# A graph kernel's third mask: one VectorE pass over the adjacency becomes an accumulating transfer from GpSimd's queue

## The reference

```python
# layer 0: attention, one head: leaky_relu(s_i + t_j), masked by adj, softmax, relu
# layer 1: 8 heads of 16, scores in leaky_relu, masked by adj, softmax, elu
# layer 2: mean over the neighbours (relation 1) @ W + x @ self_w.T + b, layernorm, relu
# layer 3, 4 heads of 32:
Wh = jnp.einsum('bsf,hfd->bhsd', features, W)
scores = jnp.einsum('bhsd,bhtd->bhst', Wh, Wh) / jnp.sqrt(jnp.float32(D))
scores = jnp.where(adj_matrix[:, None, :, :] > 0, scores, NEG_INF)
attn = jax.nn.softmax(scores, axis=-1)
h = jnp.einsum('bhst,bhtd->bhsd', attn, Wh)
```

## Time and profile before

| | |
|---|---|
| median of 3 runs | 2535.16 us (2532.8 to 2535.92) |
| the profiled execution: its time, its span | 2537.21 us, 2535.5 us |
| TensorE (PE) busy | 2281.9 us, 90% of the span |
| VectorE (DVE) busy | 2173.3 us, 86% |
| ScalarE (ACT) busy | 1944.8 us, 77% |
| GpSimd (POOL) busy | 167.5 us, 7% |
| granted TensorE clock, mean | 0.965 |
| chain that ended last | PE 64%, DVE 14%, issue 9%, ACT 8%, DMA 3%, POOL 2% |

### The profile page before, as it was taken

The page is one execution under the profiler, slowest core; times in us unless marked ns, Lnnn a source line. Parts: engine busy times, 40 slices in busy tenths (PEclk is TensorE's granted clock), DMA queues, the critical chain, the costliest instruction groups (busy, mean ns, idle before and its releaser), DMA issues.

```text
span 2535.5 us, 56744 instructions
## 1 busy us (share of the span) xinstructions
PE 2281.9 (90%) x23694; PEld 1528.0 (60%) x23813; DVE 2173.3 (86%) x4125; ACT 1944.8 (77%) x2161; POOL 167.5 (7%) x104
## 2 busy tenths in 40 slices
PE   3668999989999999999989899998989999998966
PEld 3557556575765658575665757656485765657341
DVE  3688799898988989898898989889898989989756
ACT  2758798787879878787987778788787878878714
POOL 0000001001000100100010010001001000100000
PEclk9788999999999999999999999999999999999978
DMA  6504133222323322232332123233222323101000
GB/s 129 134 18 118 42 85 77 62 74 43 102 68 85 83 65 64 43 101 68 85 84 66 62 43 101 68 85 76 60 77 42 102 68 85 45 33 52 9 17 9
DMA packets 192976, 172.80 MB, mean 68 GB/s; under 512 B 137168, under 2 KB 171088, under 8 KB 191696
## 3 DMA queue, kind: packets, MB, share of 16 engines
q1 hardware_dynamic: 191424, 135.61, 19.5%
q0 software_dynamic: 1296, 33.56, 6.5%
HBM read 151.78 MB, written 42.53 MB: 77 GB/s over the span
## 4 chain that ended last, share of the span: by engine, by line
PE 64%; DVE 14%; issue 9%; ACT 8%; DMA 3%; POOL 2%; SPq 1%; POOLq 0%; ACTq 0%; DVEq 0%
PE kp L821 15%; PE kp L804 10%; PE fp L707 9%; PE fp L646 9%; PE kp L797 6%; PE kp L752 3%; DVE weight L1317 3%; ACT ramp L994 3%; DMA shared<-shared 2%; DVE bstat L1127 2%; ACT weight L1037 2%; PE kp L749 2%; POOL bsmall L541 2%; PE fp L600 2%; PE fp L593 1%
## 5 line engine op out<-in xcount | busy, mean ns | idle before, releaser
L994 ACT ACTIVATE ramp<-s1row,tbig 128x1024 bf16<-128x1024 f32 x864 | 921.0, 1143 | 85.6 <-DVE weight L1317 85.5
L1037 ACT ACTIVATE weight<-kp,shift 128x1024 f32<-128x1024 f32 x512 | 543.9, 1114 | 196.2 <-PE kp L804 194.7
L1317 DVE TENSOR_TENSOR weight<-ramp,AT 128x2048 bf16<-128x2048 bf16 x512 | 609.6, 1221 | 75.9 <-ACT ramp L994 52.1
L821 PE MATMUL kp<-weight,w 128*33 128x512 f32 x2048 | 490.9, 600 | 9.5 <-ACT weight L1037 5.7
L707 PEld LDWEIGHTS fp<-vh_parts,weight 128*128 128x128 bf16 x8192 | 402.8, 100 | 130.5 <-DVE weight L1317 66.7
L707 PE MATMUL fp<-vh_parts,weight 128*128 128x102 bf16 x8192 | 431.9, 212 | 40.0 <-DVE vh L1325 24.7
L804 PE MATMUL kp<-shared 32*128 32x512 f32 x2048 | 298.0, 652 | 9.8 <-ACT weight L1037 7.5
L821 PEld LDWEIGHTS kp<-weight,w 128*33 128x33 f32 x2048 | 97.7, 110 | 321.4 <-issue 255.9
L646 PEld LDWEIGHTS fp<-features,weight 128*128 128x128 f32 x2048 | 234.9, 194 | 40.9 <-issue 40.3
L646 PE MATMUL fp<-features,weight 128*128 128x129 f32 x2048 | 240.7, 279 | 16.9 <-DVE weight L1228 16.9
L1456 DVE SCALAR_TENSOR_TENSOR weight<-AT,weight 128x1024 f32<-128x1024 bf16 x182 | 214.6, 1222 | 36.7 <-ACT weight L1037 36.7
(11 more groups left out here) (179 smaller groups left out, 2527.3 us busy)
## 6 DMA issues: line engine op xcount, KB each, us to landing
s1row<-s_rows_dram SPq DMA_DIRECT2D x128, 512.0 KB, 4.1
adj_bf_dram<-in_adj_dram POOLq DMA_DIRECT2D x15, 2048.0 KB, 13.7
x<-in_x_dram SPq DMA_DIRECT2D x16, 512.0 KB, 7.5
xfT<-s_row_dram SPq DMA_DIRECT2D x16, 512.0 KB, 3.6
shared<-shared SPq DMA_DIRECT2D x32, 256.0 KB, 3.5
out_dram<-elu SPq DMA_DIRECT2D x16, 512.0 KB, 4.5
adj_bf_dram<-in_adj_dram POOLq DMA_DIRECT2D x2, 1024.0 KB, 10.8
s_rows_dram<-weight SPq DMA_DIRECT2D x16, 32.0 KB
```

The costliest lines, as they stand in the source:

```text
L821: last = pe.matmul(kp[side(h), 0, :], w3[:, (2 * J + x) * H3 + h, :], weight3[:, w % P_RING, x * HALF:(x + 1) * HALF], start=(J == 0 and x ...
L994: act.activation(ramp[:, u % R_RING, :], s1row[:, h % S_RING, :], ACT.Relu, bias=tbig1[:, jt, h:h + 1], scale=BIG).then_inc(ramp_ready.sem, 1)
L1037: act.activation(weight3[:, w % P_RING, :], kp[:, 1 + 2 * (w % 2):3 + 2 * (w % 2), :].rearrange("p a n -> p (a n)"), ACT.Exp, bias=shift3[ ...
L1317: dve.tensor_tensor(edges[:, u % B_RING:u % B_RING + 2, :], ramp[:, u % R_RING:u % R_RING + 2, :], AT[:, third, jt:jt + 2, :], ALU.min).th ...
```

## The change

`layer3_mask` leaves VectorE. GpSimd issues a transfer that adds a tile of -1 (`minus`, 128x256 bf16, read over and over) to the third of `AT`, in pieces of 256 elements (512 bytes), 32 for each of 128 partitions: 4096 pieces, 2 MB written. `mask3_made` counts 16 a graph. TensorE waits for it ahead of couple 0 as before. VectorE now waits for it ahead of its first masked couple. The five couples of `MASKED` stay. All five tables of steps are new. On VectorE `stats2` goes from step 16 to 17, behind one more L1317, and `relu2` from 21 to 23, behind an L1325 as well; on TensorE the first `project0` goes from step 25 to 29, behind four more pieces of layer 1, and couple 0 of the scores keeps step 49 with the same pieces ahead of it.

```diff
+        minus = sb("minus", [P, 2 * P], BF16)
...
-        mask3_made = signal("mask3_made", 1)
+        mask3_made = signal("mask3_made", 16)
...
         ON_POOL = [
-            (dict(adjacency=3, rstd0=4, rstd1=5, rstd2=0, rstd3=1, rstd_tail=2),),
+            (dict(adjacency=3, mask3=1, rstd0=5, rstd1=6, rstd2=0, rstd3=2, rstd_tail=4),),
         ]
         ON_SP = [
-            (dict(adjacency=1, far=6, out=10, sources=[2, 3, 4, 5, 7], sources_ahead=[12, 13, 14], spread_row=9,
-                 store_row=8, store_sources=11, x=0),),
+            (dict(adjacency=4, far=5, out=10, sources=[0, 2, 3, 7, 9], sources_ahead=[12, 13, 14], spread_row=8,
+                 store_row=6, store_sources=11, x=1),),
         ]
...
+            pool.memset(minus[:], -1.0).then_inc(consts_made, 1)
...
+            def layer3_mask(b, third):
+                if b == 0:
+                    pool.wait_ge(consts_made, 4)
+                pool.wait_ge(sum2_made.sem, sum2_made.of(b))
+                pool.dma_start(AT[:, third].rearrange("p t (c n) -> p (t c) n", n=2 * P),
+                               minus[:].unsqueeze(1).broadcast_to([P, T * T // 2, 2 * P]), accum_op=ALU.add) \
+                    .then_inc(mask3_made.sem, 16)
...
+                if k is not None and s == at["mask3"]:
+                    layer3_mask(k, (r + 2) % 3)
...
-            def layer3_mask(b, third):
-
-                dve.wait_ge(sum2_made.sem, sum2_made.of(b))
-                dve.tensor_scalar(AT[:, third], AT[:, third], -1.0, None, ALU.add).then_inc(mask3_made.sem, 1)
-
             def layer3_masked(b, third, v):
...
+                    if w == 2 * masks(b)[0]:
+                        dve.wait_ge(mask3_made.sem, mask3_made.of(b))
```

More of the change, by code:

```diff
@@ L390, in graph_stack @@
         ON_PE = [
[L391 to L396, removed]
+            (dict(maxima1=93, maxima3=44, project0=[29, 31, 35], project1=91, project2=102, project3=42, scores3=[49,
+                 53, 56, 58, 64, 70, 74, 83, 85, 87, 90, 94, 98, 101, 104, 106], self2=5, self_weights=73, shift3=48,
+                 sources1=95, spread0=47, spread1=96, sum1=[18, 20, 23, 25, 26, 27, 37, 38], sum2=[0, 1, 3, 8, 9, 13,
+                 15, 16], top0=41, turn0=[17, 24], turn1=89, turn2=99, turn3=39, turn_back=30, unit0=[72, 75, 76, 78,
+                 79, 80, 81, 82], unit1=[2, 4, 6, 7, 10, 11, 12, 14, 19, 21, 22, 28, 32, 33, 34, 36, 40, 43, 45, 46,
+                 50, 51, 52, 55, 59, 60, 62, 63, 65, 66, 67, 69], values3=[54, 57, 61, 68, 71, 77, 84, 86, 88, 92, 97,
                  100, 103, 105, 107, 108]),),
@@ L399, in graph_stack @@
         ON_ACT = [
[L400 to L405, removed]
+            (dict(cut1=[81, 82], cut1_second=[87, 91], elu=66, exp3=[31, 32, 34, 36, 38, 39, 41, 42, 47, 48, 53, 54,
+                 57, 58, 62, 63, 64, 65, 68, 69, 71, 72, 74, 75, 78, 79, 84, 85, 88, 89, 92, 93], exps0=35, exps1=77,
+                 first2=86, out3=[49, 67, 83, 96], prepare0=46, project0=[16, 18, 20], project1=73, project3=26,
+                 ramps=[0, 1, -1, 2, 3, 4, -1, 5, 6, 8, 9, 11, 13, 14, 15, 19, 21, 22, 28, -1, 29, 30, -1, 33, 37, -1,
+                 40, 43, 44, 45], ramps_ahead=[94, 95], second2=90, self2=7, sources1=76, sum1=[17, 23, 24],
+                 turn0=[10, 12], turn1=70, turn2=80, turn3=25, unit0=[50, 51, 52, 55, 56, 59, 60, 61], wide3=27),),
@@ L406, in graph_stack @@
         ]
         ON_DVE = [
[L408 to L414 removed]
+            (dict(affine2=20, columns1=[91, 92], cut1=[94, 96], cut1_third=[99, 102], divide1=81, elu1=84, finish0=82,
+                 finish1=69, finish3=25, head1=[7, 13, 21, 29, 40, 49, 56, 62], lengths3=34, low2=101, masked3=[55,
+                 61, 65, 66, 70, 71, 72, 74, 75, 76, 85, 90, 93, 95, 98, 100], maxima1=87, maxima3=36, maximum0=39,
+                 most0=33, norm0=83, norm1=88, norm3=27, out2=15, prepare=68, ramps=[2, 9, 35, 44, 51], relu2=23,
+                 residual3=46, rest2=97, shift0=57, shift3=38, shifts1=89, stats2=17, tail3=60, top0=28, top1=86,
+                 unit0=[63, 64, 67, 73, 77, 78, 79, 80], unit1=[0, 1, 3, 4, 5, 6, 8, 10, 11, 12, 14, 16, 18, 19, 22,
+                 24, 26, 30, 31, 32, 37, 41, 42, 43, 45, 48, 50, 52, 53, 54, 58, 59], z0=47),),
@@ L1519, in step @@
                     layer3_residual(m)
-                if k is not None and s == at["mask3"]:
-                    layer3_mask(k, (r + 2) % 3)
                 for v in range(PAIR_UNITS):
```

7 lines of the change are left out of this document (removed).

## The result

| | before | after |
|---|---|---|
| median (lowest to highest, runs) | 2535.54 us (2532.8 to 2538.62, 4) | 2622.14 us (2620.03 to 2636.01, 4) |
| ratio to before, with its interval | 1 | 1.0353 [1.0315, 1.0391] |
| span of the profiled execution, mean granted clock | 2535.5 us, 0.965 | 2622.3 us, 0.948 |
| from the first power of layer 2 to the second, start to start | 12.32 us | 15.10 us |

The change costs 86.6 us; the forecast was 2616 us.

A forecast was written before the change was run, and what follows sets the result against it. TensorE was taken to set the time, with the landing of `spread_far` as hinge. 13 x 6.5 = 84.5 us of collision less 3.3 us of gain gave +81 us, 2616 us for the median; range 2518 to 2690 us.

The forecast's parts named there:

- What bounds the kernel: TensorE sets the time, busy 140.5 of 147 us; a later landing of `spread_far` lengthens the period by as much.
- The pass filled a hole, 0.1 us a period: VectorE without its 2.30 us mask pass would wait for ScalarE's copy `w3`, winning only 0.1 us a period.
- The new order gains at most 15 us: TensorE reaches layer 2's result sooner: 1.1 us usable in each of some 14 full periods.
- The issue, 8 us and free up to 12.7 us: GpSimd issues the mask's 4096 pieces in about 8 us; only time over 12.7 us holds VectorE at `layer2_norm`.
- X = 20 us: Duration of the mask's transfer on the DMA engines, landing 9.6 us ahead of couple 0, so TensorE doesn't wait.
- The cast queues behind the mask and reaches into `spread_far`: Load of the next adjacency, behind the mask on its queue, makes `spread_far` land 4.8 us late; chance 0.50.
- 6.5 us in 13 periods, 84.5 us: Cost of the late `spread_far`: 4.8 us of delay plus 1.7 us of lower clock in each period with a load.
- The row load and the store and spread of layer 0's row, nothing: These transfers, in the same stretch as `spread_far`, were costed at nothing, since TensorE stands still for it meanwhile.
- its issue holds GpSimd: Rival, with the mask itself late: a 20 us issue is 7.3 us over what is free, 2652 us; chance 0.20.
- Harmless and the new order gains, 2520: Rival: with X under 15 us the cast ends before `spread_far`, and 1.1 us is won in 14 periods; chance 0.22.

The follow-up runs named there:

- early cast: Load of the next adjacency right behind `rstd3` on GpSimd's queue, as in the changed kernel (2622.14 us); the kernel before with only this move: 2533.91 us.
- late cast: Changed kernel with the load of the next adjacency back behind `rstd_tail` on GpSimd's queue, all else as changed: 2566.45 us, 1.0129.

## Why the prediction was right, and where by luck

The number (2616 against 2622) is nearer than its working deserves. In steps between measured kernels: the pass gone, 2535.7 to 2528.9; the new orders, to 2521.7; the transfer behind the power, to 2566.4; the early cast, to 2622.1. That is -6.8, -7.3, +44.8 and +55.7.

- **What bounds the kernel**: right. `spread_far` is the hinge: a delay at it, or ahead of it on the chain, came out in the period, in the orders of the kernel before nearly us for us (1.87 us a graph in the powers' distance, 2.0 in the time).
- **The pass filled a hole, 0.1 us a period**: right inside the periods (147.1 against 147.2); the whole effect is 6.8 us and not 1.6.
- **The new order gains at most 15 us**: right as a bound; 7.3 us were there: 0.8 us in a full period, less a later start. The forecast counted it in three periods only, 3.3 us, since a collision hides it elsewhere.
- **The issue, 8 us and free up to 12.7 us**: wrong twice. It takes 3.19 us. The slope of 1.9 ns a row from 32 and 64 rows does not carry to 4096; over the 0.56 us issue of 64 rows it is 0.65 ns a piece. And it is not free, short as it is: VectorE's scales beside it take 1.87 us longer. This is the step that failed. I asked only how long GpSimd would be held and whether `rstd3` would be late, not what the issue does to VectorE. The Trainium skill, "SBUF — State Buffer", section "Who interferes with whom", says that the two share ports and that whoever issues first blocks the other, so that the blocking can fall on either. I had used one direction. The traces show the other: the issue takes 3.2 us beside the scales and away from them, and the scales lengthen, by 1.87 us beside an issue of 3.19, where the page has a full block. No run here shows whether the shared ports are the reason.
- **X = 20 us**: right, 20.9 (18.1 to 25.5). The store of `out`, whose pieces are the same, was the row to go by. The Trainium skill's fit in "DMA: Bandwidth & Descriptors", section "Anatomy of one DMA — SWDGE (gpsimd) path", had given an estimate of 6.8 us, and the measurement decides against it for a transfer that accumulates in pieces of 512 bytes. The mask is in time for couple 0, as forecast: nobody waits for it.
- **The cast queues behind the mask and reaches into `spread_far`**: that it reaches into it is right; that the mask alone brings it there is not shown. Counted from the first power, the forecast has the mask down at 22.6 us, the cast at 35.6 and `spread_far` at 36.6; the trace has 23.6, 33.6 and 36.7. The cast's landing comes out near by two errors: it was issued at 17.6 us and not at 14.9, and it did not wait for the mask's data to be through, since it landed 10.0 us behind them, less than the 13.2 to 13.7 us that it takes alone. `spread_far` lands 3 us behind the cast, not 1. The transfer was 4.1 us longer than before, forecast 4.8.
- **6.5 us in 13 periods, 84.5 us**: the term is too large. Its price by experiment is 55.7 us, 4.3 a period. 48.6 us more wait for `shared` than with the late cast (73.2 against 24.6) are 3.7 a period; the rest goes with the lower clock. The periods did take 154 us, but 2.0 of the 6.2 us that each of the 13 grew by are there with the late cast too (1949.6 us against 1924.3, in the slowest of its runs); they belong to the scales, to what clock goes with them, and to the new orders' gain against them.
- **The row load and the store and spread of layer 0's row, nothing**: no run took them apart. With no mask the new orders as a whole gain 7.3 us, these moves among them. Beside a cast the row load is not free: in one period with the transfer ahead of the statistics and the early cast, it landed late and held ScalarE and VectorE for 9 us.
- **The rivals**: "its issue holds GpSimd" named the right instruction and the wrong victim. "Harmless and the new order gains, 2520" is close to what no mask at all gives (2521.7), and 2526.6 can be had with the transfer.

The misses compensate: 29 us too much for the collision, 45 us not seen for the transfer behind the power (30 of them by the scales, the rest in part clock), and about 11 us of gain not counted. That is luck.

## What to carry to other kernels

A transfer that nobody waits for has two costs besides its duration: what its issue does to the instructions of another engine beside it, and what it does to the next transfers on its queue. Look at what runs beside the issue, not only at what stands behind it, and put it beside work that keeps its time (here one power earlier: 32 us). A transfer's end depends on when the new order lets it be issued, here 3.7 us later, and on what is under way ahead of it, here 2 us more, and a short transfer on the critical path that falls into it lands with or behind its end. And a period with its own first or last iteration has to be checked there too: one collision in the first graph cost 12 us.

## What was not expected of the hardware

- **GpSimd's issue slows VectorE's scale.** Of the eight 128x128 f32 `tensor_scalar` of that period the shortest takes 330 ns and the longest 1458, and the long ones are those that start while the issue runs. With the transfer ahead of the power (late cast) other VectorE work stands beside an issue at 685.08 and keeps its time: L1405, which reads PSUM, has a mean of 345 ns in that execution and 344 before.

```profile
685.28 2.16 DVE L1405 SCALAR_TENSOR_TENSOR yb<-kp,deg,yb 128x128 f32<-128x128 f32 x8
```

- **A turn (DMA transpose) beside an accumulating transfer.** Its issue takes 23 to 27 us with the mask issued 4 us ahead of it, 9 to 14 with the mask 4 us or more behind it, 9 to 12 in the same place with no mask, and in the kernel before, at another place, mostly 7.7 to 9. The mask itself lengthens from 21 to 25 us.
- **A copy of 256 KB issued together with the cast** takes 15.4 to 15.5 us instead of 3.6: it lands 0.1 and 1.7 us behind the cast's end, although the two are on different queues. Issued 1.6 us ahead of the cast it kept its time, in the one period that has this.
- **Half of the accumulating transfer takes more than half of its time**: 15.3 us for 2048 pieces of 512 bytes, 21.6 us for 4096 in the same place. Both run beside the turn of the next adjacency; in the orders of the kernel before, away from it, 4096 take 18.2 us. What the turn's share is stays open.
